# Cross stage of a decoder layer: probabilities split and transposed through SBUF and DMA instead of TensorE and PSUM

## The reference

```python
    def _L0_xattn_ref(q, k, v, attention_mask, Wq, bq, Wk, bk, Wv, bv, Wo, bo):
        N_HEADS = 16                      # D_MODEL = 512, HEAD_DIM = 32
        qm = _split_heads(q @ Wq.T + bq)
        km = _split_heads(k @ Wk.T + bk)
        vm = _split_heads(v @ Wv.T + bv)
        scores = jnp.einsum('bnlh,bnph->bnlp', qm, km) / np.sqrt(HEAD_DIM).astype(np.float32)
        scores = jnp.where(attention_mask[:, None, None, :], scores, MASK_FILL)
        attn = jax.nn.softmax(scores, axis=-1)
        out = jnp.einsum('bnlp,bnph->bnlh', attn, vm)
        out = out.transpose(0, 2, 1, 3).reshape(B, L, D_MODEL)
        return out @ Wo.T + bo
    ...
    x = x + _L0_attn_ref(_layernorm(x, axis=-1), ...)
    x = x + _L0_xattn_ref(_layernorm(x, axis=-1), ctx_1024, ctx_1024, mask_BxS2_bf1, ...)
    x = x + _L0_ffn_ref(_layernorm(x, axis=-1), ...)
```

## Time and profile before

| | us |
|---|---|
| median of three runs | 1784.48 |
| the profiled execution, its own time | 1784.44 |
| its span | 1782.6 |
| PE busy (share of the span) | 1685.4 (95%) |
| DVE busy | 1514.8 (85%) |
| ACT busy | 1069.8 (60%) |
| POOL busy | 1017.6 (57%) |
| one step of the cross stage, from scores(0) to the next scores(0), at 1187.67 | 56.98 |

### The profile page before, as it was taken

The page is one execution under the profiler, slowest core; times in us unless marked ns, Lnnn a source line. Parts: engine busy times, 40 slices in busy tenths (PEclk is TensorE's granted clock), DMA queues, the critical chain, the costliest instruction groups (busy, mean ns, idle before and its releaser), DMA issues.

```text
span 1782.6 us, 37666 instructions
## 1 busy us (share of the span) xinstructions
PE 1685.4 (95%) x13824; PEld 1392.6 (78%) x13824; DVE 1514.8 (85%) x2089; ACT 1069.8 (60%) x3420; POOL 1017.6 (57%) x721
## 2 busy tenths in 40 slices
PE   6899999999999999997799999999999999999996
PEld 5678888888888888885677787778777787777874
DVE  6788888888888888787678898888988899888886
ACT  4434444444443334442767788777877788777884
POOL 3267766666666666695554464545654465544521
PEclk9999999999999999998799999999999999999998
DMA  5410111111111111044201112011111112011101
GB/s 210 128 42 25 47 48 48 47 47 47 47 47 47 47 47 47 2 107 79 68 8 51 62 62 63 25 62 62 63 38 43 62 62 69 19 62 62 39 20 54
DMA packets 72793, 98.75 MB, mean 55 GB/s; under 512 B 22208, under 2 KB 30528, under 8 KB 72640
## 3 DMA queue, kind: packets, MB, share of 16 engines
q1 hardware_dynamic: 72064, 96.63, 17.0%
q10 hardware_dynamic: 576, 0.07, 0.0%
HBM read 59.66 MB, written 37.03 MB: 54 GB/s over the span
## 4 chain that ended last, share of the span: by engine, by line
PE 28%; ACT 12%; DVE 8%; issue 4%; DVEq 0%; POOL 0%; ACTq 0%; POOLq 0%
PE ring L1464 11%; ACT prob_c L1679 10%; DVE g_sb L1794 5%; PE sc L1492 5%; PE ring L1504 3%; PE ring L1469 3%; PE ring L1549 3%; PE sc L1484 2%; PE sc L1464 1%; DVE q_first L1975 1%; ACT relu L1660 1%; DVE g_sb L1791 1%; DVE gT L1803 1%; ACT gT L1669 1%; ACT pT L1648 0%
## 5 line engine op out<-in xcount | busy, mean ns | idle before, releaser
L447 PE MATMUL qb<-wqkv,xT 128*128 128x512 f32 x2304 | 551.9, 393 | 6.1 <-DVE wqkv L1016 6.1
L447 PEld LDWEIGHTS qb<-wqkv,xT 128*128 128x128 f32 x2304 | 429.7, 189 | 93.7 <-DVE wqkv L1016 6.3
L1679 ACT ACTIVATE prob_c<-sc,ntop 128x128 f32<-128x128 f32 x1024 | 362.6, 390 | 22.1 <-DVE ntop L1821 18.7
L1410 POOL TENSOR_TENSOR rstd<-vare,half_c 128x1 f32<-128x1 f32 x64 | 35.1, 549 | 433.6 <-DVE vare L1875 433.6
L1679 ACT ACTIVATION_READ_ACCUMULATOR prob_c<-sc,ntop 128x1 f32 x1024 | 236.1, 231 | 0.0
L352 POOL TENSOR_TENSOR prod_pool<-v,prob 128x1024 f32<-128x1024 f32 x64 | 179.9, 2810 | 67.8 <-DVE prob L911 62.6
L1464 PE MATMUL ring<-wqkv,aT_c 128*128 128x512 f32 x768 | 194.5, 402 | 8.0 <-DVE aT_c L1778 7.1
L663 ACT ACTIVATE v<-qb 128x512 f32<-128x512 f32 x64 | 38.3, 598 | 259.9 <-PE qb L447 249.6
L583 PE MATMUL ob<-wout,aT 128*128 128x512 f32 x768 | 191.4, 398 | 0.8 <-DVE aT L941 0.8
L1821 DVE TENSOR_REDUCE ntop<-sc 128x4 f32<-128x512 f32 x256 | 173.3, 683 | 12.3 <-PE sc L1492 9.5
L663 ACT ACTIVATE qk<-qb 128x512 f32<-128x512 f32 x128 | 76.1, 595 | 175.8 <-PE qb L447 175.8
(11 more groups left out here) (152 smaller groups left out, 3358.5 us busy)
## 6 DMA issues: line engine op xcount, KB each, us to landing
x_tile<-in_x SPq DMA_DIRECT2D x16, 1024.0 KB, 5.2
x_scratch<-xres SPq DMA_DIRECT2D x16, 1024.0 KB, 4.6
x_tile<-x_scratch SPq DMA_DIRECT2D x16, 1024.0 KB, 5.3
out<-x SPq DMA_DIRECT2D x64, 256.0 KB, 2.0
kt<-k_scratch SPq DMA_DIRECT2D x16, 512.0 KB, 3.2
v_c<-v_scratch SPq DMA_DIRECT2D x16, 256.0 KB, 3.6
raw<-in_wqkv SPq DMA_DIRECT2D x3, 1024.0 KB, 8.9
ctx<-in_ctx SPq DMA_DIRECT2D x1, 1024.0 KB, 8.3
```

The costliest lines, as they stand in the source:

```text
L447: last = nc.tensor.matmul(qb[g % 4][:, :], xT[p][a][:, k, t * P:(t + 1) * P], wqkv[b][:, k, c * D:(c + 1) * D], start=(n == 0), stop=(n == ...
L1679: last = nc.scalar.activation(prob[:, h, :], sc[g][:, (h % 4) * C:(h % 4 + 1) * C], ACT.Exp, bias=ntop[:, h:h + 1], accum_out=total[:, t % ...
```

## The change

- `prob_T` and all its 16 calls per step are gone from PE, with their places in the ring and ACT's and DVE's passes over the transposed banks.
- ACT now makes the high part from `prob` in SBUF to a new f16 tile `p16[0]`, eight heads (1024 columns) at a time: `prob_hi(t, 0)` between the second and the third group of exponentials, `prob_hi(t, 1)` behind the fourth.
- The low part, `prob - p16[0]`, goes to `p16[1]`, heads 0 to 7 by GpSimd (`prob_lo(t)` between its other work) and heads 8 to 15 by VectorE (`prob_lo(t)`, at the head of the next slot; that of tile 3 ahead of `norm_lo(2)`).
- SP issues two DMA transposes per tile (`turn(j, t)`), `p16[0]` to `pT[0]` and `p16[1]` to `pT[1]`, 128 x 2048 f16 each, 512 KB; `values` waits for both.
- Exponentials of a tile wait for the low parts of the tile before, which read `prob`.
- On DVE `add_attn(t)` stands behind `tops(t, 3)`, no longer ahead of it. On POOL `norm2` and `norm` change places in part. On SP the stores and `load_ctx` are ordered around `turn`.
- `g_sb` takes the place that was kept free for `bout`, so that SBUF holds the two new tiles.

The diff, cut to its core (the lines dropped are the same removal of `prob_T`, `prob_hi` and `prob_lo` in the last step's `ending` and in the ring's tables):

```diff
-        return [("out", 0), ("aT", 0), ("pv", 0), ("wo", 0), ("x2T", 0), ("pT", 0), ("pT", 1)]
...
+        return [("out", 0), ("aT", 0), ("pv", 0), ("wo", 0), ("x2T", 0)]
...
+        p16 = [sb(f"p16_{h}", [P, H, C], F16) for h in range(2)]
...
+            def turn(j, t):
+
+                n = 4 * j + t
+                for h in range(2):
+                    if h == 0:
+                        wait(sp, p_hi, 2 * (n + 1))
+                    else:
+                        wait_each(sp, (p_lo[0], n + 1), (p_lo[1], n + 1))
+                    wait(sp, psum["pv"], n)
+                    sp.dma_start_transpose(pT[h][:, :, :],
+                                           p16[h][:, :, :].rearrange("p h c -> p (h c)")).then_inc(turned[h], 16)
...
-                if active(j - 1, "out", 3):
-                    store(j - 1, 1 - p, 3)
-                for t in range(R - 1):
+                for t in range(R):
+                    if t == 3 and has(j, 1):
+                        load_ctx(j + 1, 1 - p)
                     if active(j, "out", t):
                         store(j, p, t)
-                if has(j, 1):
-                    load_ctx(j + 1, 1 - p)
+                    if has(j):
+                        turn(j, t)
 
...
+                def prob_lo(t):
+                    if not has(j):
+                        return
+                    n = 4 * j + t
+                    wait(pool, p_hi, 2 * n + 1)
+                    wait(pool, turned[1], 16 * n)
+                    nc.gpsimd.tensor_tensor(p16[1][:, 0:8, :], prob[:, 0:8, :], p16[0][:, 0:8, :],
+                                            ALU.subtract).then_inc(p_lo[0], 1)
...
                     norm(1)
+                prob_lo(0)
                 norm2(j, 1)
                 if has(j, 1):
                     norm(2)
+                prob_lo(1)
+                norm2(j, 2)
+                if has(j, 1):
                     norm(3)
-                norm2(j, 2)
+                prob_lo(2)
+                norm2(j, 3)
                 if has(j, 1):
                     residual(0)
                     residual(1)
-                norm2(j, 3)
+                prob_lo(3)
                 if has(j, 1):
                     residual(2)
                     residual(3)
...
-                    wait(pe, taken["pT"], 4 * over)
+                    wait_each(pe, (turned[0], 16 * over), (turned[1], 16 * over))
...
-                prob_T(0)
-                prob_T(1)
                 for t in (1, 2):
                     scores(t)
                     attn_T(t)
-                    prob_T(4 * t - 2)
-                    prob_T(4 * t - 1)
                     ffn_out(t)
                     out_proj(t)
                     values(t)
                     norm2_T(t)
-                    prob_T(4 * t)
-                    prob_T(4 * t + 1)
...
-                    wait(act, psum["pT"], 16 * j + 4 * t - 3 + g)
+                    wait(act, p_lo[g // 2], 4 * j + t)
...
-                def prob_hi(j, i):
-                    if not has(j):
-                        return
-                    g = i % 4
-                    if g == 0:
-                        wait(act, psum["pv"], 4 * j + i // 4)
-                    take_hi(j, "pT", i, pT[0][:, 4 * g:4 * g + 4, :])
+                def prob_hi(t, part):
+
+                    n = 4 * j + t
+                    heads = slice(8 * part, 8 * part + 8)
+                    wait(act, exped, 4 * n + 2 * part + 2)
+                    if part == 0:
+                        wait(act, turned[0], 16 * n)
+                    nc.scalar.activation(p16[0][:, heads, :], prob[:, heads, :], ACT.Copy).then_inc(p_hi, 1)
...
-                prob_hi(j - 1, 14)
-                prob_hi(j - 1, 15)
-                attn_hi(0)
-                for g in range(4):
-                    exps(0, g)
-                for t in (1, 2, 3):
-                    norm2_hi(t - 1)
-                    prob_hi(j, 4 * t - 4)
-                    prob_hi(j, 4 * t - 3)
+                for t in range(R):
+                    if t > 0:
+                        norm2_hi(t - 1)
                     attn_hi(t)
                     exps(t, 0)
                     if t == 3:
                         norm_hi(0)
-                    prob_hi(j, 4 * t - 2)
-                    prob_hi(j, 4 * t - 1)
                     exps(t, 1)
+                    prob_hi(t, 0)
                     if t == 3:
                         norm_hi(1)
                     exps(t, 2)
                     exps(t, 3)
+                    prob_hi(t, 1)
                 norm_hi(2)
                 norm_hi(3)
...
-                def prob_lo(j, i):
-                    if not has(j):
-                        return
-                    heads = slice(4 * (i % 4), 4 * (i % 4) + 4)
-                    take_lo(j, "pT", i, pT[1][:, heads, :], pT[0][:, heads, :])
+                def prob_lo(t):
+
+                    n = 4 * j + t
+                    wait(dve, p_hi, 2 * n + 2)
+                    wait(dve, turned[1], 16 * n)
+                    nc.vector.tensor_tensor(p16[1][:, 8:, :], prob[:, 8:, :], p16[0][:, 8:, :],
+                                            ALU.subtract).then_inc(p_lo[1], 1)
...
                 add_out(0)
-                prob_lo(j - 1, 14)
-                prob_lo(j - 1, 15)
                 tops(0, 0)
                 attn_lo(0)
                 tops(0, 1)
@@ -1931,31 +1922,27 @@
                 add_attn(0)
                 statistics(0)
                 for t in (1, 2, 3):
+                    prob_lo(t - 1)
                     norm2_lo(t - 1)
-                    prob_lo(j, 4 * t - 4)
                     tops(t, 0)
-                    prob_lo(j, 4 * t - 3)
                     attn_lo(t)
                     tops(t, 1)
                     if t < 3:
                         add_out(t)
                     else:
                         norm_lo(0)
-                    prob_lo(j, 4 * t - 2)
                     tops(t, 2)
-                    prob_lo(j, 4 * t - 1)
-                    add_attn(t)
                     if t == 3:
                         norm_lo(1)
                     tops(t, 3)
+                    add_attn(t)
                     if t == 3:
                         add_out(3)
                     normalise(t)
                     statistics(t)
+                prob_lo(3)
                 norm_lo(2)
                 norm_lo(3)
-                prob_lo(j, 12)
-                prob_lo(j, 13)
```

44 lines of the change are left out of this document (10 added, 34 removed).

## The result

The changed kernel takes 1872.78 us (median of four, 1869.74 to 1876.45); the kernel before, run beside it, 1784.32. The ratio is 1.0496, interval 1.0473 to 1.0520: 88.5 us slower, where 44.5 slower had been forecast. That is inside the range of 1786 to 1930 and at the upper end of the forecast's own range (1873). The sign was right, the sum only half of what came. The profiled execution is the slowest of the four; its span is 1874.7 us, against 1782.6.

The account below looks back on a forecast made before the run. A ring of ACT's exponentials and PE's scores was taken as the bound. Slot 0's 0.95, 3 x 0.60 and the tail's 0 make 2.75 us a step, 44.0 in 16, plus 1 at the end: 1829 us, range 1786 to 1930.

Parts of the forecast that it names:

- The bound and its ring: Each slot: ACT's exponentials, then PE's scores, then ACT again, with 0.32 us where PE and DVE hold it back.
- the term of slot 0: Slot 0 grows by 0.95 us, as ACT's new high part replaces no pair of copies there.
- The chain of slots 1 and 2: Exponentials wait for DVE's low part, itself 0.6 us behind POOL; slots 1 to 3 take 10.50 us, +0.60 each.
- GpSimd's low part, covered: POOL's pass of about 2.5 us ends before the next exponentials need it and costs nothing.
- The transposes, hidden: Both DMA transposes of a tile land by E + 6.3 (E: ACT's exponentials done), near plain-load speed, at no cost.
- the limit of E + 8.3: Latest landing that costs nothing, counted from the end of a tile's exponentials (E); a transpose may take 3.1 us.
- the rival's own rule: Exposed transposes, chance 0.25: if one takes D > 3.1 us, a slot takes D + 7.4; at 4.5, 1896 us.
- its own signs of being wrong: PE waits for a DMA ahead of values, DVE's pass doesn't wait for POOL, or the tail is well under 17 us.
- The upper bound of 8.6 us: Time of one transpose, from 2048 rows of 256 bytes at 0.067 us a packet on 16 engines.
- The tail at 0: Later queries against earlier hinges in the tail: no change, from -0.7 to +0.7 us a step.
- the rival by which the tail gives more than the slots take: PE alone holds the tail, so 3.2 us a step come back: 1777 us, chance 0.11.
- The clock: Rival, chance 0.08: TensorE's clock falls to 1.2 GHz, scores double, 1.9 us more per tile, 122 in all: 1951 us.

Follow-up runs that it names:

- e11: e10 with the first high part copied by VectorE ahead of add_attn instead of by ScalarE, and half as many filling transposes: 1801.8 us.
- e8: Changed kernel with the first tile's low part early, GpSimd's norm2 behind VectorE's low part, and PE's idle time filled with identity transposes: 1841.8 us.
- e10: e8 with VectorE's low part of tile 3 moved behind norm_lo(2) and norm_lo(3): 1822.7 us.
- e2: Changed kernel with GpSimd's low part of the very first tile ahead of norm(0) and norm(1), which wait for a load: 1865.0 us.
- e3: Changed kernel without any DMA transpose, values reading tiles of zeros set once and waiting only for the high and low parts: 1879.5 us.
- e1: Changed kernel with the transposes of norm2_T(0) issued five times more, in PE's idle time at the end of slot 0: 1879.3 us.
- e5: Changed kernel with unread transposes of the identity filling PE's idle stretches: 1861.0 us.
- e12: e11 with, for tile 3 alone, the first high part on ScalarE behind norm_hi(3) and GpSimd's low part behind its four residuals: 1837.8 us.
- e6: Changed kernel with GpSimd's norm2 waiting for VectorE's low part of the tile before: 1866.9 us.
- e9: Changed kernel with VectorE's low part of tile 3 behind norm_lo(2) and norm_lo(3) instead of ahead of them: 1866.2 us.
- e4: Changed kernel with low parts exchanged: VectorE takes heads 0 to 7 behind the fourth maximum, GpSimd heads 8 to 15 behind the last exponentials: 1889.8 us.

## Why the forecast came out as it did

**The bound and its ring: right.** The exponentials waited for `ntop` behind DVE's low part, slots grew although PE and DVE were relieved, and slot 0 grew by 1.01 (forecast 0.95). e11 confirms the term of slot 0 by taking it away.

**The chain of slots 1 and 2: right in kind.** Counted from the first matmul of the scores, S, the exponentials were forecast at S + 3.90. Slot 1: S + 4.30 (1241.51 - 1237.21), for the pass was held up by 0.78, not 0.60, and began 0.24 later. Slot 2: S + 3.67, for it was not held up at all, but began 0.39 later, 0.15 of it behind the statistics. Of the other 0.24, in both slots, 0.11 is the copy ahead of it, which takes its full 1.06 us and not 0.95. From there both need 6.83 us to the next scores, 0.23 more than the forecast's 6.60; the copies don't start as closely behind the exponentials as the old ones. Sums 11.13 and 10.50. That slot 2 came out as forecast is luck: 0.60 too much for a wait that wasn't there, 0.62 too little for the rest. The wait behind GpSimd is not an average over slots: it is all there in slot 1 and absent in slot 2, and e8 shows it to be worth 0.74 in slot 1. And with no wait at all a slot is 10.36 (e8, e10), where the forecast's own sum gives 9.90.

**GpSimd's low part, covered: right in the steady steps, wrong at the start.** Step 0 came out 12.2 us over its share of the sum (14.9 less 2.75). 7.0 of it is the load that GpSimd's queue had to wait for ahead of the first low part (e2); the other 5.1 were not taken apart, but with GpSimd's `norm2` waiting and PE filled as well, step 0 falls to 62.52 (e8).

**The transposes, hidden: right, shown by e3, but by a hair.** The pair lands at the limit of E + 8.3 that had been worked out: E + 1.1 and 6.8 us give E + 7.9 in the median, E + 8.4 in the slot shown. By the rival's own rule a transpose of more than 3.1 us was exposed, and 4.6 gave slots of 12.0; that rule put the two one behind the other (2D), where the trace has them overlap. What the forecast had wrong is the landing: it had both land within 6 us, and of its own signs of being wrong the first, "PE waits for a DMA ahead of `values`", did occur, in 18 slots for up to 1.8 us; e3 shows how little that cost. The second, that DVE's pass doesn't wait for POOL, holds in slot 2 and not in slot 1. The upper bound of 8.6 us took too much for a short row: by the page 338304 - 72064 = 266240 packets came, 2080 a transpose, and took (0.364 x 1874.7 - 0.170 x 1782.6) x 16 / 266240 = 0.023 us each, not 0.067.

**The tail at 0: off by a little.** At full clock slot 3 and tail take 28.99 us after (ten steps), against 28.23 + 0.60 forecast; the tail alone is 17.84 in the step shown, against 17.43, so the rival by which the tail gives more than the slots take is out. That the low part ahead of `norm_lo` delays the queries was named in the prediction, and e10 measures it as 1.22 us a step in that kernel.

**The clock: the rival was half true.** It had a chance of 0.08 as a fall in every slot at 122 us. What came is a fall in slot 1 of nearly every step, where it costs 0.2, and in slot 3 of some, which take 1.6 to 3.7 us more each (30.56 to 32.64 against 28.99). "Slot 0 now holds 1.00" did not exclude it; what differs in the trace is PE's idle time in one piece of 2.5 us. Filling that piece held the clock in nine of 14 slots 1 (e1), filling all held it everywhere (e5); which pause brings which fall stays open, and e12's two slots show that the length of the last one does not settle it. It is 12 to 15 of the missing 44 us (e5), and it can hide what other repairs bring (e6, e9).

So what was mis-sized is the sum's 2.75 us a step: 4.86 was measured. Two terms of it failed, the clock that was put at nothing and the chain of slot 1 (its wait, the full copy ahead of it and the longer rest). Of the 2.11 between, 1.08 is the clock; 0.65 is slot 1 at full clock (11.16 against 10.51) and 0.38 slot 3 and tail (29.21 against 28.83). 2.11 x 14 = 29.5, with 12.2 of step 0 and 5.5 behind the last regular step make 47.2, which is the 47.1 by which the span missed the forecast's 1827.6. Most of the last 5.5 us lies behind the last tile's scores, where the kernel takes 5.8 us longer than before and the forecast had put 1: PE waits 2.70 us for the last transposes there, and over the last tile's slot (1814.93 to 1834.89) the mean granted clock is 0.83, where it was 1.00 before.

```profile
1834.89 1.38 PE L1565 MATMUL ring<-v_c,pT 128*128 128x32 f16 x48 [2.70 <-issue]
```

e10's 1822.7 is near the 1829, but it doesn't confirm the sum: there the pass takes 1.22 or 1.23 us in slots 1 and 2 of all regular steps, unhindered, and for that case the prediction has 1801. The 22 us between are again the slots of 10.36 instead of 9.90, step 0 and the ending. And the range held for other reasons than it was made for: its upper part was to cover slower transposes and a clock low in every slot, and it was filled by the terms above.

## What to carry to other kernels

Before work is taken off an engine, look for the ring that closes the slot: taking 64 transposes a step from beside the exponentials gave back nothing that shows, while ScalarE's copy of 1.06 us between them cost 1.0 a slot (e11) and VectorE's pass of 1.22 ahead of the next maxima 0.5, or 1.3 when it took 2.00 (e4). Where PE was near full load, new idle time on it came with a lower clock here; a repair should be timed with PE's clock held, or its gain may be lost to the clock and be judged wrongly: e6's edit could not be told from nothing alone, and is worth 0.74 us in each slot 1 with PE filled. A pass on an engine that shares with GpSimd is priced by what GpSimd does at that moment: write down both queues side by side, the first step included, before moving it.

## What was not expected of the hardware

- A 128x2048 f16 DMA transpose within SBUF lands after 4.6 us (4.3 to 6.8) and holds the issuing queue for 2.1 us in the median, 4.1 to 5.7 for a pair in the regular steps: x1's load in the tail is issued 5.0 us after the start of the pair before it.
- The same 1024 columns from SBUF: f32 to f16 copy 0.68 us on VectorE, 1.06 on ScalarE; subtraction 1.22 on VectorE, 2.13 on GpSimd; beside GpSimd 1.38 for the copy and up to 3.03 for the subtraction (step 0 of e11).
- Transposes that nobody reads made the kernel 11.8 us faster; the clock stood at 1.00 in every slot of steps 1 to 14 with them, and below 0.95 in 20 without.
